# A fused transformer kernel: another order for the shared expert's products around the last gate, and other PSUM banks for its outputs

## The reference

```python
scores = sigmoid(x @ gate_w.T) + bias              # 16 experts
topk_w, topk_idx = top_k(scores, 4)
cw = weights of the four, divided by their sum, spread over the 16 experts
out = sum over experts e of cw[:, e] * ((silu(x @ Wg[e].T) * (x @ Wu[e].T)) @ Wd[e].T)
out = out + (silu(x @ Sg.T) * (x @ Su.T)) @ Sd.T   # the shared expert, 256 wide, for every row
return rows + out
```

## Time and profile before

| | |
|---|---|
| median of 3 runs | 665.66 us (664.49 to 668.22) |
| the profiled execution's own time | 667.79 us |
| its span, first to last instruction | 666.0 us |
| TensorE busy | 649.7 us, 98% of the span |
| VectorE, ScalarE, GpSimd busy | 307.5, 244.9, 175.1 us |
| granted TensorE clock, mean | 0.997 of full speed |

### The profile page before, as it was taken

The page is one execution under the profiler, slowest core; times in us unless marked ns, Lnnn a source line. Parts: engine busy times, 40 slices in busy tenths (PEclk is TensorE's granted clock), DMA queues, the critical chain, the costliest instruction groups (busy, mean ns, idle before and its releaser), DMA issues.

```text
span 666.0 us, 9684 instructions
## 1 busy us (share of the span) xinstructions
PE 649.7 (98%) x2275; PEld 380.0 (57%) x2276; DVE 307.5 (46%) x746; ACT 244.9 (37%) x755; POOL 175.1 (26%) x227
## 2 busy tenths in 40 slices
PE   9999999999999999999999999998999999999994
PEld 6565444456766776677776567574444444444441
DVE  3996223533343345476665765255333333333332
ACT  5575522212255454647567474320111111111110
POOL 2356100101000000004414335463123332333244
PEclk9999999999999999999999999999999999999998
DMA  9999999332422242123425437415777758868655
GB/s 336 405 421 419 421 421 435 142 112 79 157 77 84 69 162 72 63 80 128 142 73 169 159 108 274 106 75 172 226 186 158 142 88 197 188 130 241 117 75 68
DMA packets 83925, 119.45 MB, mean 179 GB/s; under 512 B 9728, under 2 KB 52096, under 8 KB 83360
## 3 DMA queue, kind: packets, MB, share of 16 engines
q1 hardware_dynamic: 52640, 88.17, 36.6%
q0 software_dynamic: 8816, 18.00, 14.0%
q10 hardware_dynamic: 22432, 12.85, 6.8%
HBM read 54.73 MB, written 64.39 MB: 179 GB/s over the span
## 4 chain that ended last, share of the span: by engine, by line
PE 87%; DVE 4%; DMA 3%; another core or an unknown queue 2%; issue 1%; ACT 1%; POOL 0%; POOLq 0%; SPq 0%; DVEq 0%; ACTq 0%
PE ps L1350 56%; PE ps L1550 9%; PE ps L1535 4%; PE ps L1514 4%; PE ps L1461 3%; PE ps L1471 3%; PE ps L1462 3%; PE ps L1336 2%; DMA out<-rq,sidx 1%; PE ps L1483 1%; PE ps L1366 1%; PE ps L1397 1%; DMA kv<-probabilities 1%; DMA r<-in_ctxT 1%
## 5 line engine op out<-in xcount | busy, mean ns | idle before, releaser
L1350 PE MATMUL ps<-kv,rq 128*128 x432 | 192.4, 594 | 0.5 <-ACT rq L912 0.5
L1350 PE MATMUL ps<-zT,r 128*128 128x256 f32 (+1 forms) x552 | 132.5, 395 | 0.5 <-ACT kv L812 0.5
L1350 PEld LDWEIGHTS ps<-kv,rq 128*128 128x128 f32 x432 | 78.9, 190 | 87.4 <-issue 87.0
L1350 PEld LDWEIGHTS ps<-zT,r 128*128 128x128 f32 x552 | 103.4, 190 | 23.9 <-issue 10.1
L1550 PE MATMUL ps<-r 128*128 128x512 f32 x192 | 85.3, 593 | 0.0
L702 POOL DMA_INDIRECT out<-rq,sidx x36 | 56.6, 1573 | 98.6 <-DMA out<-rq,sidx 66.5
L619 POOL TENSOR_SCALAR ve<-mv 128x1 f32<-128x1 f32 x32 | 7.1, 223 | 248.1 <-DVE mv L1071 248.1
L1275 DVE TENSOR_TENSOR rq<-ps,rq 128x256 f32<-128x256 f32 x36 | 15.3, 425 | 100.7 <-ACT rq L916 95.5
L916 ACT ACTIVATE rq<-ps 128x256 f32<-128x256 f32 x36 | 13.8, 383 | 120.6 <-PE ps L1350 114.5
L1550 PEld LDWEIGHTS ps<-r 128*128 128x128 f32 x192 | 35.1, 190 | 37.8 <-issue 37.8
L850 ACT ACTIVATE r<-ps,snm 128x128 f32<-128x128 f32 x128 | 45.2, 365 | 21.7 <-DVE snm L1187 18.5
(11 more groups left out here) (189 smaller groups left out, 824.5 us busy)
## 6 DMA issues: line engine op xcount, KB each, us to landing
slot_rows<-rq SPq DMA_DIRECT2D x4, 8192.0 KB, 49.2
kv<-in_experts SPq DMA_DIRECT2D x54, 256.0 KB
rq<-slot_rows ACTq DMA_DIRECT2D x138, 64.0 KB
probabilities<-r SPq DMA_DIRECT2D x31, 256.0 KB
late<-probabilities SPq DMA_DIRECT2D x64, 64.0 KB
r<-in_Wq SPq DMA_DIRECT2D x1, 3072.0 KB, 20.7
r<-in_Wo SPq DMA_DIRECT2D x2, 1536.0 KB, 6.5
kv<-probabilities SPq DMA_DIRECT2D x44, 64.0 KB
```

The lines of the kernel that those rows point to most:

```text
L1350: mm = pe.matmul(out, lhs(k), rhs(k), start=(k == 0), stop=(k == n - 1))
```

## The change

The order of the steps between the last two gates and the expert stage is rewritten, and with it:

- SiLU: none is taken before the last gate's exp any more. `sh_silu` 0 and 1 move behind it, and the SiLU and multiply of products 4 to 7 become a step of their own, `sh_act` 2 and 3.
- TensorE: `sh_gu` 4, 5, 6 and 7 now stand one by one between the steps of the last two gates and places; no `sh_d` stands there any more.
- `sh_d` 0 to 4 follow `count`, ahead of `tables`; `sh_d` 5 to 7 follow `tables`.
- the outputs of `sh_d` go to banks 6, 7, 4, 5, 0, 6, 2, 3 in place of 6, 7, 6, 7, 6, 7, 0, 1, with waits to match. `sh_d` 2 to 5 all wait for the third multiply, since banks 4 and 5 hold products 4 and 5 until then.
- VectorE's `turn(0, 0)` moves from ahead of the add of block 4 to ahead of the add of block 2.
- the first tiles of the expert stage now wait for adds of `sh_d`: `gate_up(0)` for three, `gate_up(1)` for four, the first transposes for seven and eight.

```diff
--- before.py
+++ after.py
@@ -429,11 +429,11 @@
                 prog.append(("front",))
 
         prog += [("sh_gu", 3), ("pv", NU - 1), ("ln_t", 3, J - 2), ("op0", J - 1), ("gate", J - 2), ("gate_v", J - 2)]
-        prog += [("sh_silu", a) for a in range(EARLY // 2)]
-        prog += [("op1", J - 1), ("ln_stat", 3, J - 1), ("place", J - 2), ("sh_gu", 4), ("ln_z", 3, J - 1), ("sh_d", 0),
-                 ("ln_t", 3, J - 1), ("sh_d", 1), ("gate", J - 1), ("gate_v", J - 1), ("sh_gu", 5), ("place", J - 1),
-                 ("count",), ("route", 0), ("sh_gu", 6), ("route", 1), ("sh_d", 2), ("sh_d", 3), ("sh_gu", 7), ("tables",),
-                 ("sh_d", 4), ("sh_d", 5), ("sh_d", 6), ("sh_d", 7)]
+        prog += [("op1", J - 1), ("ln_stat", 3, J - 1), ("sh_gu", 4), ("place", J - 2), ("ln_z", 3, J - 1), ("sh_gu", 5),
+                 ("ln_t", 3, J - 1), ("sh_gu", 6), ("gate", J - 1), ("gate_v", J - 1), ("sh_silu", 0), ("sh_silu", 1),
+                 ("sh_act", 2), ("sh_gu", 7), ("place", J - 1), ("count",), ("route", 0), ("route", 1), ("sh_d", 0),
+                 ("sh_act", 3), ("sh_d", 1), ("sh_d", 2), ("sh_d", 3), ("sh_d", 4), ("tables",),
+                 ("sh_d", 5), ("sh_d", 6), ("sh_d", 7)]
 
         def off_pe(layer, j):
 
@@ -491,7 +491,7 @@
 
         def shared_down(j):
 
-            return ps[:, (6 if j < J - 2 else 0) + j % 2, :]
+            return ps[:, (6, 7, 4, 5, 0, 6, 2, 3)[j], :]
 
         @block.sync
         def _(sp):
@@ -894,11 +894,11 @@
                     if i < EARLY:
                         act.wait_ge(s_hg, i + 1)
                         act.copy(graw[:, i, :], shared_bank(i)).then_inc(s_hraw, 1)
-                    elif i % 2 == 0:
-                        a = i // 2
-                        act.wait_ge(s_hg, i + 1)
-                        act.wait_ge(s_hz, a - 1)
-                        act.activation(shg[a % 2], shared_bank(i), ACT.Silu).then_inc(s_hsil, 1)
+                elif kind == "sh_act":
+                    a = step[1]
+                    act.wait_ge(s_hg, 2 * a + 1)
+                    act.wait_ge(s_hz, a - 1)
+                    act.activation(shg[a % 2], shared_bank(2 * a), ACT.Silu).then_inc(s_hsil, 1)
                 elif kind == "sh_silu":
                     a = step[1]
                     act.wait_ge(s_hraw, 2 * a + 1)
@@ -1254,15 +1254,14 @@
                     dve.wait_ge(s_hsil, a + 1)
                     dve.wait_ge(s_hraw, 2 * a + 2)
                     dve.tensor_tensor(zs[:, a, :], graw[:, 2 * a + 1, :], shg[a], ALU.mult).then_inc(s_hz, 1)
-                elif kind == "sh_gu" and step[1] >= EARLY and step[1] % 2:
-                    i = step[1]
-                    a = i // 2
+                elif kind == "sh_act":
+                    a = step[1]
                     dve.wait_ge(s_hsil, a + 1)
-                    dve.wait_ge(s_hg, i + 1)
-                    dve.tensor_tensor(zs[:, a, :], shared_bank(i), shg[a % 2], ALU.mult).then_inc(s_hz, 1)
+                    dve.wait_ge(s_hg, 2 * a + 2)
+                    dve.tensor_tensor(zs[:, a, :], shared_bank(2 * a + 1), shg[a % 2], ALU.mult).then_inc(s_hz, 1)
                 elif kind == "sh_d":
                     j = step[1]
-                    if j == J - 4:
+                    if j == 2:
                         turn(0, 0)
                     if j == J - 1:
                         turn(1, 1)
@@ -1599,15 +1598,15 @@
                     pe.matmul(ps[0:6, 1, 0:ENTRIES], cols[:, :], ident[:, 0:ENTRIES], start=True, stop=True).then_inc(s_tabt, 1)
                 elif kind == "sh_d" and step[1] < J - 1:
                     j = step[1]
-                    pe.wait_ge(s_hz, j // 2 + 1)
+                    pe.wait_ge(s_hz, 3 if 2 <= j < 6 else j // 2 + 1)
                     if j == 0:
                         pe.wait_ge(s_ws[2], 16)
                         pe.wait_ge(s_oc, NU)
                         pe.wait_ge(s_x3, J)
-                    if 2 <= j < J - 2:
-                        pe.wait_ge(s_x4, j - 1)
-                    if j == J - 2:
+                    if j == 4:
                         pe.wait_ge(s_trc, len(TRN))
+                    if j == 5:
+                        pe.wait_ge(s_x4, 1)
                     dense(shared_down(j), lambda c: shared_act(j, c),
                           lambda c: wsh[:, (KC + c) * D:(KC + c + 1) * D], I // P).then_inc(s_hd, 1)
 
@@ -1660,15 +1659,18 @@
                 gate_up(i, par, load, at)
 
             pe.sem_inc(s_ed, 1)
+            pe.wait_ge(s_x4, 3)
             gate_up(0, 0, *first)
             load, at = load_of(1), slot_of(1)
+            pe.wait_ge(s_x4, 4)
             gate_up(1, 1, load, at)
+            pe.wait_ge(s_x4, J - 1)
             act_in(0, 0, 0)
             load, at = load_of(2), slot_of(2)
             old = slot_of(0)
             gate_up(2, 0, load, at)
+            pe.wait_ge(s_x4, J)
             act_in(1, 1, 0)
-            pe.wait_ge(s_x4, J)
             down(0, 0, 0, old)
 
             pe.wait_ge(s_idl, 16)
```

## The result

| | before | changed |
|---|---|---|
| median | 665.77 us (664.49 to 668.22, 6 runs) | 669.59 us (668.25 to 671.38, 6 runs) |
| profiled execution | 667.79 us, span 666.0 | 668.33 us, span 666.6 |

The timed runs say 3.8 us slower: ratio 1.0056, 95% interval 1.0035 to 1.0076. The two profiled executions lie only 0.5 us apart. That disagreement is the core of this case.

What follows compares the result with a forecast made beforehand. TensorE, busy 649.7 of 666.0 us, was taken as the bound. `gate_up(0)` starting 2.3 us later, including a 2.1 us hold, was added to the timed median 665.66: 668.0 us, range 664.6 to 670.0.

Steps and rivals of the forecast that it cites:

- main case: Gate 7's increment held 2.1 us, so `gate_up(0)` starts 2.3 us later than before: 668.0 us, chance 0.42.
- rival C: Late increments belong to the profiled execution only; `gate_up(0)` at 462.7 against 458.9, +3.8 us: 669.5 us, chance 0.07.
- the late increments: TensorE's signals for gate 6, `sh_gu` 5 and place 7 reaching consumers 2.8 to 4 us late, near GpSimd's row-number scatters.
- t: Time of ScalarE's exp of gate 7: 439.27 before, forecast 442.3 without a hold, 444.4 with one.
- the worked chain: Steps timed from gate 7's exp: slots +5.2, table +13.6, `gate_up(0)` +20.4 us, with stalls on TensorE.
- The 3.6 us of idle time: TensorE's idle time at place 6, `tables` and the next down products; the most to win, 0.5% of the time.
- The hold on gate 7: Gate 7 ends inside block 6's row-number scatters, so its exp was forecast 2.1 us late; bounds 0.04 to 4.0 us.
- case A: No hold, gate 7 taken at once; `gate_up(0)` at 462.7, +0.2 us: 665.9 us, chance 0.27.

Runs made afterwards that it cites:

- before_again: The kernel before, unedited, timed and profiled a second time; median 664.70 us, ratio 0.9998.
- before_third: The kernel before, unedited, with a third profile on a third chip; ratio to its other runs 1.0002.
- banks_only: The kernel before with the new banks for the down products and the new waits, order of steps unchanged; ratio 0.9999.
- gate_first: The changed kernel with `sh_gu` 6 behind the last gate instead of ahead of it; ratio to the kernel before 1.0044.
- gate_place_first: As gate_first, with place 7 and `count` also ahead of `sh_gu` 7; ratio to the kernel before 1.0007.
- turned_early: As gate_place_first, with `sh_gu` 5 behind the last transposes, `ln_z` 7 and place 6 moved, place 7 and `count` ahead of `sh_act` 2; ratio 0.9998.

## Why the prediction was right in its number and wrong in its main case

The forecast was 668.0 in a range up to 670.0, and within 0.5% at 0.70. Measured was 669.59, inside the range, but slower by 0.56% with an interval from 0.35% to 0.76%; slower by over 0.5% had 0.26. The shift is that of rival C, which I gave 0.07: +3.8 us forecast, +3.8 measured. Its sum is right, its premise only in part: the late increments are no matter of profiling as such, since 11 other profiled executions had none.

**What held.** With t = 442.80, the changed trace follows the worked chain, each row within 0.3 us: stall before `sh_gu` 6 0.77 (0.8 forecast); SiLUs end at t + 2.64 (2.6); `sh_d` 0 at t + 3.94 (3.9), idle 0.36 (0.5); `pos` at t + 4.47 (4.5); slots at t + 5.2 (5.2); first scatter at t + 6.37 (6.35); table at t + 13.6 (13.6), idle 0.88 (1.1); idle before `sh_d` 5 0.44 (0.6); load chain 12.67 (12.7); `gate_up(0)` at t + 20.47 (20.4), idle 0.73 (0.9). The distance without a hold was forecast at 462.7 - 424.13 = 38.57 and is 38.64. The releasers are the ones named. The table loads: one is left, and the SiLU starts 1.29 us behind its start, as in the earlier trace rows, with nothing more between them. Nothing on TensorE waited for the two that went, and no run removes them alone.

**What failed, first: the reference.** I took 462.50 as the start of `gate_up(0)` before. It was read correctly, from an execution whose increments came late. Without them it is 34.79 us behind op1 7, or 458.9 in that trace's times, the very figure of C. The 3.6 us of idle time that "there is to win" did not exist in either repeat. That this execution lay 2.1 us above its median was no proof either way: the profiled executions of before_again, before_third and banks_only lie 1.3, 1.4 and 2.0 us above theirs, and have no late increment and a distance of 34.79. What marks the first trace alone are starts released by `remote`, as the profile writes it where it names no engine: three in the earlier trace rows, and none in the waits of any other trace.

**Second: the hold on gate 7.** The 2.1 us that I added to t, and with them the idle time before place 7 and the late exp, did not come. The condition that I had set for it was met: the scatters of row numbers of block 6 began at 440.14, the gate ended inside them at 442.76, and exp came at 442.80. So the step from "inside the scatters" to "held" is what failed. By my own list that is case A, whose 665.9 is as wrong, since A keeps the held reference. In the profiled pair A is even what is seen: 463.27 against 462.50, of which 0.50 us is op1 7's later start, so +0.3. The two errors, -3.6 and +2.1, partly cancelled. That the number came near is luck.

**Where the 3.85 us are.** Against the second trace of before, all from the start of op1 7: exp of gate 7 at 18.17 in place of 13.69, 4.5 us later, since three blocks of products and the stall for `zT` stand ahead of it in place of one block and two down steps. `pos` at 22.64 in place of 17.28, 5.4 later: place 7 ends 4.5 later, and the third SiLU on ScalarE adds 0.9. No run takes this SiLU away alone. The turn ends at 37.92 in place of 32.26 (its row is below), 5.7 later. Before, 2.5 us of cover lay between the turn's end and `gate_up(0)`; now there is none, and an add of 0.7 us more: 5.66 - 2.53 + 0.72 = 3.85. The load took 0.2 of the 5.66. The down products under the route do not help: TensorE's work is the same, and what ends last is the chain from gate to loaded rows. The second trace of before, VectorE:

```profile
456.50 0.71 DVE L1051 STREAM_TRANSPOSE rq<-rq 128x512 f32<-128x512 f32 x1 [3.05 <-DMA rq<-slot_rows]
```

gate_first and gate_place_first bear this out in two steps: the gate alone gives back 0.9 of the 3.85, gate and place together 2.9, and turned_early, with the copy of `zT` covered, the last 0.9.

## What to carry to other kernels

Before idle time in one profile is counted as winnable, profile the same kernel again, above all if an engine starts microseconds late with no engine named as the releaser. Where an engine is 98% busy, a chain that runs beside it (here gate, place, scatter, load, turn) has a length and a limited cover, here 2.5 us: work that is moved ahead of the chain's head uses the cover up, and what goes beyond it shows in the time (5.7 us later against 2.5 us of cover here). An earlier head helps only as long as no other queue, here GpSimd's scatters of the block before, is then the last to be ready. An instruction that waits for a DMA belongs behind everything that another engine needs from that queue; the same move cost at most 0.4 us in one order and about 3 us in another.

## What the runs showed of the hardware

The late increments, 2.8 to 4.0 us, stood in one of 12 profiled executions. Scatters of row numbers alone do not cause them: the kernel before had them in flight in two more profiled executions, and the changed kernel in two, with no late increment. What does cause them, and whether some timed runs have them, stays open; no run here shows it. Nor is it settled why the span behind `gate_up(0)` differs between executions (203.3 us in the first trace of the changed kernel, 204.7 in its second). That is why a difference of under 1 us is read here from the distance and not from a single time.
